# Attention steps of a layer kernel: narrow bank transposed first, score products split over the step, normalising on three engines

## What is computed

```
x = x + tanh(g_xattn) * moe(layernorm(x), ids)
h0 = layernorm(x)
attn = attention(rmsnorm(h0, ln1), Wq, Wk, Wv, Wo)      # 16 heads of 32, causal softmax over 512 keys
mod  = 0.1 * tanh(attn @ A)                             # A: 512 x 16
h    = rmsnorm(h0, ln2)
gate = silu(h @ W_in.T + mod * (h @ A) @ B)
y    = h0 + gate * (h @ W_up.T) @ W_down.T              # 2048 wide
x = x + tanh(g_ffn) * y
```

## Time and profile before

| | us |
|---|---|
| median of three runs (1060.45 to 1062.85) | 1061.8 |
| the profiled run, timed | 1061.96 |
| its span in the trace | 1059.8 |
| PE busy in the span | 1033.5 |
| DVE busy | 722.4 |
| ACT busy | 589.6 |
| POOL busy | 252.1 |

### The profile page before, as it was taken

One profiled execution on the slowest core, in us unless ns is written; L12 is line 12 of the kernel. 1 busy time (PEld: TensorE's weight loads), 2 busy tenths in 40 slices (PEclk: granted clock), 3 DMA queues, 4 the chain that ended last, 5 costly groups with the idle time before them and its releaser, 6 DMA issues.

```text
span 1059.8 us, 17623 instructions
## 1 busy us (share of the span) xinstructions
PE 1033.5 (98%) x5336; PEld 853.5 (81%) x5337; DVE 722.4 (68%) x1661; ACT 589.6 (56%) x1399; POOL 252.1 (24%) x252
## 2 busy tenths in 40 slices
PE   6999999999999999999999999999999999999998
PEld 6787878877888878878888888778888888788887
DVE  7766756996665559985665479966655599854443
ACT  4464546886434447875444368864344478753342
POOL 4536123641000115640000136410001155300000
PEclk9999999999999999999999999999999999999999
DMA  6534133443222416343322354432234253322221
GB/s 239 201 141 161 49 117 74 96 110 134 90 89 91 147 47 173 69 127 129 106 90 89 111 141 98 113 130 90 89 91 147 63 157 80 95 86 89 89 89 50
DMA packets 47084, 115.93 MB, mean 109 GB/s; under 512 B 6800, under 2 KB 6800, under 8 KB 46096
## 3 DMA queue, kind: packets, MB, share of 16 engines
q1 hardware_dynamic: 43968, 105.06, 33.2%
q0 software_dynamic: 3040, 9.96, 2.7%
HBM read 76.46 MB, written 13.37 MB: 85 GB/s over the span
## 4 chain that ended last, share of the span: by engine, by line
PE 86%; DVE 8%; issue 3%; DMA 1%; ACT 1%; SPq 0%; DVEq 0%; POOL 0%; POOLq 0%
PE bank L518 67%; PE bank L721 5%; PE bank L735 4%; DVE wr L1329 3%; PE bank L684 3%; DVE nb L1341 2%; PE bank L688 1%; PE bank L770 1%; DMA stack<-wr 1%; PE bank L574 1%; PE bank L589 1%; DVE big L1350 1%; PE bank L632 1%; SPq L312 0%; ACT wr L887 0%
## 5 line engine op out<-in xcount | busy, mean ns | idle before, releaser
L518 PE MATMUL bank<-hT,wr 128*128 128x512 f32 x1488 | 358.4, 390 | 0.0
L518 PEld LDWEIGHTS bank<-hT,wr 128*128 128x128 f32 x1488 | 278.8, 188 | 60.0 <-issue 1.3
L518 PE MATMUL bank<-wr,actr 128*128 128x512 f32 (+1 forms) x1224 | 303.1, 397 | 2.4 <-DVE actr L1311 1.5
L518 PEld LDWEIGHTS bank<-wr,actr 128*128 128x128 f32 x1224 | 228.8, 190 | 51.1 <-issue 3.3
L491 POOL TENSOR_SCALAR big<-big,rr 128x128 f32<-128x128 f32 (+1 forms) x128 | 138.9, 1094 | 131.7 <-DVE rr L1346 131.2
L1380 DVE SCALAR_TENSOR_TENSOR wr<-stream,lns,wr 128x256 fp32r<-128x256 f32 x256 | 121.7, 536 | 51.0 <-ACT wr L1006 51.0
L972 ACT ACTIVATE big<-bank,nb 128x512 f32<-128x512 f32 (+3 forms) x256 | 131.7, 527 | 27.9 <-DVE nb L1341 27.7
L430 POOL TENSOR_TENSOR wqs<-wstage,wqs 128x512 fp32r<-128x512 f32 x32 | 43.0, 1353 | 436.8 <-ACT wqs L887 435.4
L1329 DVE TENSOR_TENSOR wr<-bank,wr 128x512 fp32r<-128x512 f32 (+1 forms) x224 | 124.5, 600 | 22.2 <-ACT wr L887 22.2
L887 ACT ACTIVATE wr<-bank 128x512 fp32r<-128x512 f32 (+1 forms) x224 | 106.0, 538 | 52.9 <-PE bank L518 30.1
L887 ACT ACTIVATE actr<-act_sb 128x512 fp32r<-128x512 f32 x64 | 40.4, 632 | 145.7 <-DVE act_sb L1394 145.7
(11 more groups left out here) (180 smaller groups left out, 1039.6 us busy)
## 6 DMA issues: line engine op xcount, KB each, us to landing
stream<-in_wmlp SPq DMA_DIRECT2D x64, 512.0 KB, 4.0
stack<-wr SPq DMA_DIRECT2D x192, 128.0 KB, 2.3
stream<-in_wmlp SPq DMA_DIRECT2D x64, 256.0 KB, 2.7
big<-in_x SPq DMA_DIRECT2D x4, 1024.0 KB
big<-y_rows SPq DMA_DIRECT2D x4, 1024.0 KB, 5.5
residual<-big SPq DMA_DIRECT2D x4, 1024.0 KB
big<-residual SPq DMA_DIRECT2D x4, 1024.0 KB, 5.6
out<-big SPq DMA_DIRECT2D x3, 1024.0 KB, 4.5
```

The lines of the kernel that those rows point to most:

```text
L518: mm = pe.matmul(dst, lhs(pl, k), rhs(pr, k), start=start and i == 0, stop=stop and i == n - 1, skip_group_check=skip)
```

## The change

`NORM_DVE` is now row tile 3 alone, ACT scales row tile 0 (`normalise` in the ACT list, after the first copy of each step), POOL scales 1 and 2. The transposes go in the order 2, 1, 3, 0, bank 6 first; copies, low halves and attend products follow that order. `scores` is cut in three: the first product (row tile 3) of head n+4 stands at the end of step n, behind the attend products and the half projection, which is now last in the step instead of first; the middle ones of head n+3 stand between the transposes of tiles 3 and 0, and the second behind tile 0. Attend waits for each bank by itself. On ACT the high half of the values stands before the copies, on POOL the weights before the scaling. The values' banks are exchanged, (4, 6) to (6, 4).

```diff
-VALUES, LOW_RANK = (4, 6), 5
+VALUES, LOW_RANK = (6, 4), 5
-NORM_DVE, NORM_POOL = (3, 1), (0, 2)
+NORM_DVE, NORM_ACT, NORM_POOL = 3, 0, (1, 2)
+TURN_ORDER = (2, 1, 3, 0)
+TURNED_BANKS = ((6, 256, 1024), (5, 512, 512), (4, 512, 0))
+PART_OF = {2: 1, 1: 2, 3: 2, 0: 3}
...
+            def scores_last(n, par, loads, first=False):
                 pe.wait_ge(stk[par], loads)
                 if not first:
                     pe.wait_ge(exp_ok, n * 4 - 3)
-                rows(3, True)
+                score_rows(par, 3, True)
                 mask(0, 3 * P, 1)
+
+            def scores_middle(n, par, first=False):
                 if not first:
                     pe.wait_ge(exp_ok, n * 4 - 1)
-                rows(2, True)
-                rows(0, False)
+                score_rows(par, 2, True)
+                score_rows(par, 0, False)
                 mask(1, 2 * P, 2)
+
+            def scores_second(n, par, first=False):
                 if not first:
                     pe.wait_ge(exp_ok, n * 4)
-                rows(1, True)
+                score_rows(par, 1, True)
                 mask(2, P, 1)
...
             def head_step(b, q, j):
-                if j == 0 and q < NQ - 1:
-                    project(b, q + 1, 1, half=1)
-                elif j and q < NQ - 2:
-                    project(b, q + 2, (0, 0, 1)[j - 1], half=(0, 1, 0)[j - 1])
+                if j == 0:
+                    pe.wait_ge(vst_lo, b * NQ + q + 1)
                 if head < H - 1:
-                    turn_probs(n + 1, (j + 1) % 2)
+                    wait_probs(n + 1)
+                    for kt in (2, 1, 3):
+                        turn_tiles(n + 1, other, kt)
                 if head < H - 3:
-                    m = b * (H // 2) + q * 2 + (j + 3) // 2
-                    scores(n + 3, (j + 1) % 2, m * 48 + 48)
-                attend(b, q, n, j)
+                    scores_middle(n + 3, other)
+                if head < H - 1:
+                    turn_tiles(n + 1, other, 0)
+                if head < H - 3:
+                    scores_second(n + 3, other)
+                for kt in TURN_ORDER:
+                    if kt != 3:
+                        pe.wait_ge(pt_lo, n * 3 + PART_OF[kt])
+                    attend(kt, HI)
+                    mm = attend(kt, LO)
+                mm.then_inc(pv_done, 1)
+                if head < H - 1:
+                    project_part(b, head + 1)
                 if UP_FROM <= head < H - 1:
...
                     up_part(0, head - UP_FROM)
+                if head < H - 4:
+                    scores_last(n + 4, j % 2, stack_loads(b, head + 4))
...
+                wait_probs(b * H)
                 pe.wait_ge(vpa_ok, b + 1)
+                turn_tiles(b * H, 0, 2, first=True)
                 pe.wait_ge(ha_ok, b + 1)
-                turn_probs(b * H, 0, first=True, values_out=b + 1)
-                scores(b * H + 2, 0, b * (H // 2) * 48 + 96)
+                turn_tiles(b * H, 0, 1, first=True)
+                turn_tiles(b * H, 0, 3, first=True)
+                pe.wait_ge(vpb_ok, b + 1)
+                turn_tiles(b * H, 0, 0, first=True)
+                scores(b * H + 2, 0, stack_loads(b, 2))
                 project(b, 1, 1, half=0)
+                project_part(b, 0)
+                scores_last(b * H + 3, 1, stack_loads(b, 3))
...
+            def normalise(n, par):
+                act.wait_ge(rr_ok, n + 1)
+                rows = prob_rows(par, NORM_ACT)
+                a.activation(rows, rows, ACT.Copy, scale=rr[:, par, NORM_ACT:NORM_ACT + 1]).then_inc(pn_act, 1)
...
-                for i, (bk, w, at) in enumerate(((4, 512, 0), (5, 512, 512), (6, 256, 1024))):
-                    act.wait_ge(p_turned, n * 3 + i + 1)
-                    copy(pts[:, j % 2, HI, at:at + w], bank[bk][:, 0:w]).then_inc(pt_hi, 1)
                 if q == 0 and j == 0:
                     values_high_of(b, 0)
                 elif j == 2 and q < NQ - 1:
                     values_high_of(b, q + 1)
+                for i, (bk, w, at) in enumerate(TURNED_BANKS):
+                    act.wait_ge(p_turned, n * 3 + i + 1)
+                    copy(pts[:, j % 2, HI, at:at + w], bank[bk][:, 0:w]).then_inc(pt_hi, 1)
+                    if i == 0 and (q < NQ - 1 or j < QH - 1):
+                        normalise(n + 1, (j + 1) % 2)
```

More of the change, by code:

```diff
@@ L676, in project, with score_rows @@
                     mm.then_inc(qk_done, 1)
-            def scores(n, par, loads, first=False):
-                pe.wait_ge(stk[par], loads)
-                def rows(qt, start):
-                    bk, col, _ = SCORE[qt]
-                    w = P * (qt + 1)
-                    pe.matmul(bank[bk][:, col:col + w], stack[:, par, 0, qt * P:qt * P + P],
-                              stack[:, par, 1, 0:w], start=start, stop=False, skip_group_check=True)
-                def mask(bk, at, n):
-                    pe.matmul(bank[bk][:, at:at + P * n], identr[:, :], maskr[:, 0:P * n],
-                              start=False, stop=True, skip_group_check=True).then_inc(s_done, 1)
+            def score_rows(par, qt, start):
+                bk, col, _ = SCORE[qt]
+                w = P * (qt + 1)
+                pe.matmul(bank[bk][:, col:col + w], stack[:, par, 0, qt * P:qt * P + P],
+                          stack[:, par, 1, 0:w], start=start, stop=False, skip_group_check=True)
@@ L692, in scores, with mask @@
+            def mask(bk, at, n):
+                pe.matmul(bank[bk][:, at:at + P * n], identr[:, :], maskr[:, 0:P * n],
+                          start=False, stop=True, skip_group_check=True).then_inc(s_done, 1)
+            def scores_last(n, par, loads, first=False):
+                pe.wait_ge(stk[par], loads)
                 if not first:
                     pe.wait_ge(exp_ok, n * 4 - 3)
-                rows(3, True)
+                score_rows(par, 3, True)
                 mask(0, 3 * P, 1)
+            def scores_middle(n, par, first=False):
@@ L726, in attend @@
-            def attend(b, q, n, j):
-                pe.wait_ge(pt_lo, n * 3 + 3)
-                pe.wait_ge(vst_lo, b * NQ + q + 1)
-                for kt in range(TT):
-                    _, _, at = TURNED[kt]
-                    w = S - kt * P
-                    for part in (HI, LO):
-                        at_row = 64 * (j // 2) + R * (j % 2)
-                        mm = pe.matmul(bank[ATT][0:3 * R, kt * P:S], vst[:, q % 2, kt, at_row:at_row + 3 * R],
-                                       pts[:, j % 2, part, at:at + w], start=False, stop=False, skip_group_check=True)
-                mm.then_inc(pv_done, 1)
@@ L739, in head_step, with scores, turn @@
-            def head_step(b, q, j):
-                n = (b * NQ + q) * QH + j
-                head = q * QH + j
+            def scores(n, par, loads, first=False):
+                scores_last(n, par, loads, first)
+                scores_middle(n, par, first)
+                scores_second(n, par, first)
+            def turn(n, par, kt, qt):
+                bk, col, _ = TURNED[kt]
+                src = SCORE[qt][2] + kt * P
+                mm = pe.transpose(bank[bk][:, col + (qt - kt) * P:col + (qt - kt) * P + P],
+                                  prob[par][:, src:src + P], ident[:, :])
+                if qt == TT - 1 and kt != 1:
+                    mm.then_inc(p_turned, 1)
@@ new lines, in turn_tiles, with wait_probs, stack_loads @@
+            def turn_tiles(n, par, kt, first=False):
+                if not first and kt != 3:
+                    pe.wait_ge(pt_lo, (n - 1) * 3 + PART_OF[kt])
+                for qt in range(kt, TT):
+                    turn(n, par, kt, qt)
+            def wait_probs(n):
+                pe.wait_ge(pn_ok, n + 1)
+                pe.wait_ge(pn_act, n + 1)
+                pe.wait_ge(pn_pool, (n + 1) * len(NORM_POOL))
+            def stack_loads(b, head):
+                return (b * (H // 2) + head // 2) * 48 + 48
@@ L745, in head_step, with project_part @@
+            def project_part(b, head):
+                q, j = head // QH, head % QH
                 if j == 0 and q < NQ - 1:
@@ L1054, in batch @@
                 split_qk(b, 1, 0)
+                normalise(b * H, 0)
                 for q in range(NQ):
@@ L1347, in normalise @@
                 dve.wait_ge(rr_ok, n + 1)
-                for qt in NORM_DVE:
-                    rows = prob_rows(par, qt)
-                    v.tensor_scalar(rows, rows, rr[:, par, qt:qt + 1], None, ALU.mult).then_inc(pn_ok, 1)
+                rows = prob_rows(par, NORM_DVE)
+                v.tensor_scalar(rows, rows, rr[:, par, NORM_DVE:NORM_DVE + 1], None, ALU.mult).then_inc(pn_ok, 1)
             def values_low_of(b, q):
```

34 lines of the change are left out of this document (15 added, 19 removed).

## The result

The changed kernel takes 1064.85 us (median of 11 runs, 1062.89 to 1066.2) against 1061.52 for the kernel before beside it: 1.0031 of it, 95% interval 1.0021 to 1.0040. It is slower, by 3.3 us. The forecast was 1065.5. The number held; the sum behind it did so only in part.

A forecast was written before the change was run, and what follows sets the result against it. PE was taken to bound steps 0 to 8, DVE those from 9 on. Per batch 0.24 + 0.35 + 0.68 + 0.85 - 1.2 = +0.92, four batches +3.7: 1065.5 us against the median, range 1056.5 to 1070.

The forecast's parts named there:

- Bank order at head 0: First transposes of a batch: four instead of two stand behind DVE's copy of the values, +0.24 us a batch.
- a low half that ends 2 us earlier: Under costs nothing: the swapped value banks wait for a low half that ends 2 us earlier; cost 0.
- Head 4: First score product at the end of step 0 waits for its stack DMA; PE loses 0.5 against 0.16, +0.35 us.
- head 8: First score product at the end of step 4: stack lands at A(4)+2.11, wanted at A(4)+1.43, stall 0.68 us.
- head 12: First score product at the end of step 8: stall of 2.1 us, step 5.3 against 4.45, +0.85 us.
- The plain steps: Steps 0 to 8 without stack stalls: PE runs without a gap, reordering neither shortens nor costs; 4.64 us kept, 0.
- steps 1 to 7 aren't 4.64 apart: Sign that the forecast is wrong: steps 1 to 7 not following each other every 4.64 us.
- The tail: Steps from 9 on: DVE falls from 4.14 to 3.76 a step, ACT at 3.83 becomes slowest; -1.2 us a batch.
- second rival: Tail at PE's pace: stalls +2.12, but DVE and ACT get ahead and six steps gain 2.2; 1061.7 us, chance 0.24.
- The wait for POOL in the tail: Sign that the forecast is wrong: the wait in the tail, steps from 9 on, being for POOL.
- The rival in which the stacks come in time: Issues move up by about 1.1 us, heads 4 and 8 stall no more, head 12 costs 1.0; 1056.5 us, chance 0.23.
- ACT replaces DVE: Rival for the tail: scaling costs ACT 0.6 instead of 0.29, its step stays 4.14; 1070.3 us, chance 0.13.

The follow-up runs named there:

- late_wait: Changed kernel with step 0's wait for DVE's low half of the values moved back from before the transposes to before attend; 1064.49 us.
- best: late_leads and late_wait together, on the changed kernel; 1052.22 us, ratio 0.9904 to the kernel before.
- late_leads: Changed kernel with the first and middle score products of heads 4, 8 and 12 put back behind all ten transposes; 1053.61 us, ratio 0.9923.
- three_norm: Kernel before with only the scaling changed, spread over DVE (tile 3), ACT (0) and POOL (1, 2); 1059.72 us, ratio 0.9985.
- old_norm_swap: leads_old_norm with POOL scaling its two tiles before splitting the projection weights in step 1 of each group; 1058.52 us, ratio 0.9976.
- early_first: Kernel before with only head n+4's first score product moved to the end of step n, behind attend and the half projection; 1073.17 us.
- filled_gap: Changed kernel with nine zero-adding products of 512 columns at the end of step 8, before head 12's first score product; 1062.37 us, ratio 1.0010.
- leads_old_norm: late_leads with the old scaling on two engines (DVE two tiles, POOL 128 and 384 columns, none on ACT); 1067.70 us, ratio 1.0051.

## Why the prediction was right, and where its sum was not

The forecast of +3.7 us was the sum of terms for one batch, times four. Against batch 0 of the table, term by term:

- **Bank order at head 0, +0.24: measured +0.63** (7.03 to 7.66). The rest is the wait for the values' low half, which the change moved from attend to the transposes of step 0. The prediction let it cost nothing ("a low half that ends 2 us earlier"); at head 0 that low half is late. late_wait takes off 0.47 and leaves +0.16 for the bank order itself, for my 0.24. It matters in best; in the changed kernel the next stack wait would have stood there instead.
- **Head 4, +0.35: +0.26** (4.80 to 5.06), **head 8, +0.68: +0.90** (4.65 to 5.55), **head 12, +0.85: +0.89** (4.45 to 5.34). The mechanism, the places and their order hold. PE stood 0.31, 0.79 and 1.93 us where I had put 0.5, 0.7 and 2.1, and late_leads shows that it is the place of the product and nothing else. Head 4 came out lower only because head 0's wait had used up some of its time: with that wait gone, in late_wait, it costs 0.74 (4.80 to 5.54) and PE stands 0.79. I sized head 8 against steps of 4.64; against the 4.53 that a plain step takes now, its stall is 1.02.
- **The plain steps, 0: -0.12 each, -0.70 for six.** "Nothing moved inside such a step makes it shorter" was wrong, and "steps 1 to 7 aren't 4.64 apart" was one of the signs I had named for being wrong: they are 4.53 apart. By starts, from S(6) to S(7) of batch 0, attend is 1.14 us for 1.18, the projection 1.36 for 1.43, the transposes and scores together 1.99 for 2.02. The scaling has no part in it (three_norm keeps 4.64), the order has all of it (old_norm_swap has 4.53), and early_first, with the projection and the first score product moved, gets half (4.58). Why the same products take less time in another order isn't shown.
- **The tail, -1.2: -1.66.** I had put ACT at 3.83 a step and it is PE's 3.73; ACT is at 94%, where I had it near 100, and DVE at 93%, where I had it below 90. Of the 1.66, 0.31 is what ACT and DVE gain while PE stands at head 12, the second rival's mechanism at a seventh of its size: without that stall, in late_leads, the tail is 19.80, which is -1.35 and near my term. The wait for POOL in the tail, another of my signs for being wrong, is there once a batch (0.42 us before the transposes of head 15 in batch 0). POOL's pair takes 2.44 us for 2.17, 0.27 more, where I had 0.15. And the reason I gave, DVE's 4.14 falling with the scaling, was half a reason: DVE was full, as I had read, but three_norm gives it room and keeps 4.14, since in the old order PE and DVE then wait for each other.
- **The clock, not in the sum: +1.6 in each of two of the four batches of this trace.** I worked out 2.1 us of idle PE and did not ask what the clock does behind it.

For a batch without a fall the terms measured sum to 0.63 + 0.26 - 0.70 + 0.90 + 0.89 - 1.66 = +0.32 (0.28 by the start of PE's next work), where I had +0.92. Four such batches are +1.3, and filled_gap, the changed kernel without the falls, is 0.6 over the kernel before beside it. The other 2.5 us or so are at least in part the clock's; the two falls of the profiled execution are 3.2. So the forecast of 1065.5 stands on right stalls, two gains that I had too small (-0.70 and 0.46 of the tail) and two costs that I had left out (the moved wait and the clock). That these nearly cancelled is luck: the sum foresaw the stalls, but not how close its total would come. The second rival's 1061.7 is nearer to filled_gap's 1062.4 than my forecast is.

The rival in which the stacks come in time is out: head 8's first issue came 1.39 us ahead of the end of attend (205.17, and attend from 205.41 to 206.56 by starts), near the 1.45 of before. That ACT replaces DVE is out: ACT is at 94%, its scaling takes 397 ns.

The Trainium skill's page "SBUF — State Buffer", section Who interferes with whom, which I had weighed for POOL's scaling, turned out to matter for DVE. It says that a two-port DVE tensor_scalar and a GpSimd instruction shut each other out for the whole instruction, and that the order of issue decides who waits. The trace of leads_old_norm bears it out where POOL comes first: DVE's second scaling starts behind the start of POOL's subtraction and ends just behind its end. It bears it out for POOL's first scaling too, in direction: 128 columns take 0.95 us beside DVE's and 0.64 at the eight places where DVE's was all but over, and the 256 columns of the changed kernel take 1.22 and 0.92. So 0.3 us of it is wait, where the prediction had some 0.4, and 0.64 is work, where it had 0.52. It does not fit everywhere: in the kernel before, DVE's second scaling runs beside POOL's first and still takes 462 ns, and in leads_old_norm it ends 0.15 us behind the subtraction, less than the 0.46 that it takes alone.

## What to carry to other kernels

A product moved ahead of its old place asks that its load moves too: before moving it, set landing against new place for every head, and leave behind those with nothing to spare (here 3 of 16, worth 11 us). Each wait on PE of about 2 us has to be priced twice, once as itself and once for a slower clock that may follow (1.6 us, behind half of them here). Two edits on a loop of two engines can be worth little alone and much together, so an ablation of one says little of the pair.

## What the runs showed of the hardware that I had not expected

- **The clock falls behind 1.8 to 2.1 us of idle PE, but not each time.** In the traces of the changed kernel, late_wait and early_first, 6 of 12 such waits (1.84 to 2.09 us) were followed by a stretch at 1.2 GHz that cost about 1.6 us; none of the shorter ones in heads 4 and 8 (up to 1.16 us) was. Length doesn't tell the six from the other six: 1.84 had a fall behind it, 1.98 in batch 1 of the changed kernel had none. What does stays open.
- **DVE's scaling is held up by POOL's cast and subtraction**: 0.72 and 1.37 us instead of 0.49 and 0.46, at eight places, 8.0 us in all by the traces of leads_old_norm and old_norm_swap (9.2 by their medians). No wait list names it, since DVE counts as busy; only the duration of one instruction beside its fellows gives it away.
